# A two-layer attention kernel: the second layer's first key block in two stages, and two key maxima of each first-layer block moved to another PSUM bank

## What is computed

```python
# cross-attention of the first layer; the second has no mask
q = split_heads(query @ Wq.T + bq)
k = split_heads(context @ Wk.T + bk)
v = split_heads(context @ Wv.T + bv)
scores = einsum('bhqd,bhkd->bhqk', q / 4, k) + (1.0 - mask) * -10000.0
out = einsum('bhqk,bhkd->bhqd', softmax(scores), v)
```

## Time and profile before

| | |
|---|---|
| median of 3 runs | 1073.76 us (1072.72 to 1075.67) |
| the profiled execution's own time | 1068.03 us |
| its span | 1066.3 us |
| first layer's blocks 0 to 12 | 38.0 to 478.45 us |
| second layer's pairs of maxima | 556.69 to 573.85 us |
| second layer's blocks 14 to 27 | 575.90 to about 1013 us |

### The profile page before, as it was taken

One profiled execution on the slowest core, in us unless ns is written; L12 is line 12 of the kernel. 1 busy time (PEld: TensorE's weight loads), 2 busy tenths in 40 slices (PEclk: granted clock), 3 DMA queues, 4 the chain that ended last, 5 costly groups with the idle time before them and its releaser, 6 DMA issues. The chain is left out here.

```text
span 1066.3 us, 30777 instructions
## 1 busy us (share of the span) xinstructions
PE 1017.6 (95%) x12921; PEld 687.8 (65%) x12921; DVE 743.1 (70%) x1715; ACT 679.0 (64%) x953; POOL 420.8 (39%) x374
## 2 busy tenths in 40 slices
PE   8899999999999999998878899999999999999876
PEld 5466666676666666665544566667676666666665
DVE  4888888888888888876357666556665565566465
ACT  3677777777778777876542555566556666555722
POOL 4368888888888988881000000101100101000000
PEclk9999999999999999999998999999999999999999
DMA  8420122201221112112031010111100111000000
GB/s 313 140 71 20 54 70 71 67 23 53 71 72 34 45 65 70 53 66 93 10 120 68 2 36 2 37 36 37 36 8 30 37 37 36 2 2 2 2 1 5
DMA packets 14682, 53.31 MB, mean 50 GB/s; under 512 B 3025, under 2 KB 4817, under 8 KB 13649
## 3 DMA queue, kind: packets, MB, share of 16 engines
q1 hardware_dynamic: 14544, 51.35, 14.0%
HBM read 51.21 MB, written 0.13 MB: 48 GB/s over the span
## 5 line engine op out<-in xcount | busy, mean ns | idle before, releaser
L756 DVE TENSOR_REDUCE tile_max<-ps_max 128x1 f32<-128x448 f32 x339 | 200.7, 620 | 150.7 <-PE ps_max L1081 146.5
L753 DVE CUSTOM_DVE_ANT_0 unread<-ps_max,masks 128x448 bf16<-128x448 f32 x396 | 231.4, 621 | 67.4 <-PE ps_max L1081 66.2
L426 POOL TENSOR_TENSOR probs<-probs,masks 128x512 f32<-128x512 f32 x182 | 228.1, 1275 | 72.0 <-ACT probs L539 70.5
L551 ACT ACTIVATE probs<-ps_scores 128x1024 f32<-128x1024 f32 x193 | 187.2, 1021 | 86.2 <-PE ps_scores L1122 86.1
L546 ACT ACTIVATE probs<-probs 128x1024 f32<-128x1024 f32 x196 | 207.4, 1058 | 54.5 <-DVE probs L811 45.7
L1122 PE MATMUL ps_scores<-q_pad,k_full 32*128 32x256 f32 x3088 | 230.6, 377 | 0.0
L1139 PE MATMUL ps_out<-probs,values 128*32 128x128 f32 x6272 | 214.5, 277 | 0.7 <-ACT probs L551 0.4
L1139 PEld LDWEIGHTS ps_out<-probs,values 128*32 128x32 f32 x6272 | 159.4, 110 | 51.7 <-issue 48.0
L1122 PEld LDWEIGHTS ps_scores<-q_pad,k_full 32*128 32x128 f32 x3088 | 191.4, 186 | 0.7
L1081 PE MATMUL ps_max<-k_high,q_high 32*128 32x448 bf16 x735 | 180.1, 358 | 7.9 <-DVE tile_max L756 5.3
L1064 PE MATMUL ps_proj<-ctx_t,wk 128*128 128x448 f32 x384 | 168.8, 562 | 0.0
(11 more groups left out here) (258 smaller groups left out, 914.4 us busy)
## 6 DMA issues: line engine op xcount, KB each, us to landing
ctx_t<-in_ctx_t SPq DMA_DIRECT2D x28, 896.0 KB, 5.3
masks<-in_mask_n SPq DMA_DIRECT2D x14, 448.0 KB, 3.4
masks<-in_mask_t SPq DMA_DIRECT2D x14, 448.0 KB, 3.5
room_w<-in_L_attn_f_w SPq DMA_DIRECT2D x2, 1024.0 KB, 7.5
room_w<-in_L_ffn_w SPq DMA_DIRECT2D x2, 1024.0 KB, 8.8
room_w<-in_L_ffn_w_gate SPq DMA_DIRECT2D x1, 1024.0 KB, 10.6
room_w<-in_L_ffn_w_up SPq DMA_DIRECT2D x1, 1024.0 KB, 13.1
room_w<-in_L_ffn_w_down SPq DMA_DIRECT2D x1, 1024.0 KB, 15.0
```

The costliest lines, as they stand in the source:

```text
L426: nc.gpsimd.tensor_tensor(p, p, three(mask_t[m % 2], TILES)[:, t, :].unsqueeze(1).to_broadcast([P, 4, P]), ALU.add).then_inc(sig("bias_add ...
L551: nc.scalar.activation(prob(T, half), scores_half(T, half), ACT.Exp).then_inc(sig(f"exp_done{half}"), 1)
L753: ins = v.tensor_tensor_reduce(unread[:, j % 2, :], max_bank(m, j)[:, 0:HALF], mask_n[m % 2][:, HALF * half:HALF * (half + 1)], 1.0, -3e38 ...
L756: ins = v.tensor_reduce(tile_max[:, h, half:half + 1], max_bank(m, j)[:, 0:HALF], AX_X, ALU.max)
```

## The change

1. **Two stages in block 14.** `SPLIT` = 3: tiles 0 to 2 (384 keys) are a stage of their own, tiles 3 to 6 the next. The order of block 14's maxima is changed so that all heads' products with the first half of the keys (448 keys, which hold the first three tiles) come first. Only these, eight pairs, run before the first scores; a pair is now two heads with the same half. The other sixteen follow one by one in tiles 0 and 1 (3, 3, 2 a tile), then a second `chain` (end of tile 1) and `turn_max`/`rows_out` (tile 2), before tile 3's scores. The stage's sums go through `sums_out`, `turn_sums` and `add_sums` in tiles 3 and 4. Block 15's maxima are made in tiles 2 to 5 (9, 9, 8, 6), and block 16's as before. Where three maxima lie behind the scores, the first uses `ps_proj`. The counts of stages (`stage`, `tiles_to`, `STAGES_OF`) take the place of the counts of blocks in the waits. The idle matmuls among the pairs are left out.
2. **First layer.** One maximum behind the weighing is taken out of tile 0 and out of tile 2, and one is put behind the scores of tile 5 and of tile 6, in `ps_proj`. DVE reads these two after it has added the mask (`late_bank`, `before_mask`). In block 12, which makes no maxima in tile 6, and in block 0, whose tiles 0 to 5 have counts of their own, only a part of this applies.

```diff
+SPLIT = 3
...
+        def stage(m, t=0):
+            return m + int(m > NB or m == NB and t >= SPLIT)
+
+        def in_stage(m, t):
+            return t - SPLIT if m == NB and t >= SPLIT else t
+
+        def tiles_to(s):
+            return TILES * (s + 1) if s < NB else TILES * NB + SPLIT if s == NB else TILES * s
...
+        STAGES_OF = ((0, NB), (NB, BLOCKS + 1))
...
+        def chained(m, t):
+            return NB + 1 if m == NB and t == SPLIT - 2 else stage(m + 1) if t == CHAIN_AT and m % NB + 1 < NB else None
+
+        def rowed(m, t):
+            return NB + 1 if m == NB and t == SPLIT - 1 else stage(m + 1) if t == ROWS_AT and m % NB + 1 < NB else None
...
-            return c, half, zz, g
+            return (half, c, zz, g) if m == NB else (c, half, zz, g)
...
-        SCORED_AT = ((2, 0, 2, 1, 2, 0, 0), (2, 1, 2, 2, 2, 2, 2))
-        WEIGHED_AT = ((1, 2, 1, 2, 1, 2, 2), (0, 2, 1, 1, 0, 1, 0))
+        SCORED_AT = ((2, 0, 2, 1, 2, 1, 1), (2, 1, 2, 2, 2, 2, 2))
+        WEIGHED_AT = ((0, 2, 0, 2, 1, 2, 2), (0, 2, 1, 1, 0, 1, 0))
+
+        def late_bank(m, t):
+            return m < NB and t >= LAST_AT
+
+        def before_mask(m, t, count):
+            return 0 if late_bank(m, t) else count if m == 0 or m >= NB else min(count, 1)
...
+            if m == NB:
+                own = (3, 3, 2) if t < SPLIT - 1 else own
+                now = ((0, 0, 0), (0, 0, 0), (3, 3, 3), (3, 3, 3), (2, 3, 3), (3, 3, 0), (0, 0, 0))[t]
...
-                            if m > 0 and k == 0 and len(here) == 2 and i == 0 and (t != SUMS_AT or m == NB):
+                            if i == 0 and (two or k == 0 and (late_bank(m, t) or m == NB and t == TILES - 1) or len(here) == 3):
                                 MAX_BANK[to, j] = 2
...
-                    for i in range(H):
+                    for i in range(H // 2):
                         pair_maximum(NB, i)
                         if i in BESIDE_AT:
                             beside_in(BESIDE_AT.index(i))
-                        elif i > 5:
-                            idle_products(1, ps_out)
```

More of the change, by code:

```diff
@@ L187, in count_at @@
             l, n = divmod(m, NB)
-            now, ahead = (0, 0, 0), (0, 0, 0)
+            own, now, ahead = (0, 0, 0), (0, 0, 0), (0, 0, 0)
             first, middle = SCORED_AT[l][t], WEIGHED_AT[l][t]
[L190 to L194, removed]
+            if m == NB:
+                own = (3, 3, 2) if t < SPLIT - 1 else own
+                now = ((0, 0, 0), (0, 0, 0), (3, 3, 3), (3, 3, 3), (2, 3, 3), (3, 3, 0), (0, 0, 0))[t]
+            elif n == 0:
+                now = (2, 2, 2) if t < LAST_AT else (0, 2, 0) if t == LAST_AT else now
+            elif n + 1 < NB and t <= LAST_AT:
+                now = (first, middle, 2 if t < LAST_AT else 0)
             if n + 2 < NB:
                 ahead = (0, 0, 2) if t == LAST_AT else (first, middle, 2) if t > LAST_AT else ahead
-            return now, ahead
+            return own, now, ahead
         MAXIMA, MAX_BANK, MAX_AFTER = {}, {}, {}
         for l in range(2):
-            done, read = {NB * l: 2 * H}, {bank: 2 * H * (NB * l + 1) for bank in range(2)}
+            done = {NB * l: (2 * H, H)[l]}
+            read = {bank: 2 * H * NB * l + (2 * H, H)[l] for bank in range(2)}
             turn_of = 0
@@ L869, in _ @@
                             bias_first(m, t)
-                        for k, j in behind_scores[len(early):]:
+                        for k, j in behind_scores[early:]:
                             maximum(k, j)
-                        if t == SUMS_AT and n > 0:
-                            add_sums(m - 1)
+                        if in_stage(m, t) == SUMS_AT and stage(m, t) > STAGES_OF[l][0]:
+                            add_sums(stage(m, t) - 1)
                         if m == BLOCKS - 1 and t == SUMS_AT:
@@ L1080, in maximum, with pair_maximum @@
                     pe.wait_ge(sig("max_free"), MAX_AFTER[m, j])
[L1081 to L1088, removed]
+                product(m, j, max_bank(m, j))
+            def pair_maximum(m, i):
+                if i == 0:
+                    pe.wait_ge(sig("k_high"), 2 * m + 2)
+                if i == 2:
                     pe.wait_ge(sig("q_copied"), 4)
[L1090 to L1093, removed]
+                need("max_free", 2 * H * m + 2 * (i - 2))
+                for k in range(2):
+                    product(m, 2 * i + k, pair_bank(i)[:, k, :])
             def scores(m, t):
                 T = TILES * m + t
+                if in_stage(m, t) == 0:
+                    pe.wait_ge(sig("max_copied"), stage(m, t) + 1)
                 if t == 0:
-                    pe.wait_ge(sig("max_copied"), m + 1)
                     pe.wait_ge(sig("k_copied"), 4 * m + 4)
@@ L1117, in scores @@
                     rows = slice(32 * g, 32 * (g + 1))
-                    mm(banks[g], minus16[rows, :], max_rows[m % 2][rows, :], start=True, stop=True)
+                    mm(banks[g], minus16[rows, :], max_rows[stage(m, t) % 2][rows, :], start=True, stop=True)
                 for c in range(DC):
```

103 lines of the change are left out of this document (58 added, 45 removed).

## The result

The changed kernel takes 1061.85 us in the median of six runs (1060.48 to 1066.93) against 1073.24 us (six runs) before. The comparison gives a ratio of 0.9909 (not the quotient of the two medians, which is 0.9894), with a 95% interval of 0.9884 to 0.9935. That is faster, as forecast, but by about three times the forecast amount: 1070.0 us was expected, and the range ended at 1063.5. The profiled execution took 1060.48 us, with a span of 1058.7 us.

A forecast was written before the change was run, and what follows sets the result against it. PE was taken to bound the first layer's tiles, DVE those of the second layer's first block. Minus 5.6 plus 1.9 gave minus 3.7 us against the 1073.76 us median: 1070.0 us, range 1063.5 to 1078.0.

The forecast's parts named there:

- The second part: Second layer's first block: shorter head minus 8.6, longer tiles plus 4.5, falls of the clock plus 6.0, sum plus 1.9 us.
- First layer, minus 5.6 us.: Blocks 0 to 12: tiles 0 and 2 save 0.38 us each, tile 6 pays 0.29; minus 5.6 us in all.
- Rivals 3 and 4: First layer: 3, late ACT exponential cancels gain, 1079.2 us, chance 0.09; 4, half the tiles' gain, 1074.6 us, chance 0.18.
- The head, minus 8.6.: Before block 14's first scores: eight of sixteen paired maxima leave, saving 8.6 us.
- Tiles with eight take 5.1 us and with nine 5.7: Block 14's tiles, bound by DVE: times by number of maxima at full clock, block 36.4 us, plus 4.5.
- I take two falls, 6.0 us: Block 14: the clock falls twice to its lower level, 10 us and 3.0 us of cost each, plus 6.0 us.
- Rival 1: Block 14: no fall of the clock, second part minus 4.1 us, whole kernel 1064.1 us; chance 0.20.
- Rival 2: Block 14: lower clock holds through tiles 1 to 6, costing 13.8 us, whole kernel 1077.9 us; chance 0.08.

The follow-up runs named there:

- two_banks: Changed kernel, but block 14's groups of three maxima behind the weighing and ahead of the next tile use two banks, not three: 1063.45 us, one run.
- filled: Changed kernel plus idle PE products before the maxima are turned and behind five later maxima of block 14's tile 0: 1060.92 us, ratio 0.9895.
- threes_0_4: Changed kernel, first layer: tile 4's maximum behind the weighing goes behind its scores, tile 6's behind tile 0's scores: 1065.49 us, ratio 0.9940.
- stages_only: Changed kernel with the first layer's tables of before, so only block 14's two stages: 1067.74 us, ratio 0.9948.

## Why the prediction was wrong

The direction was right, but only the first layer carried it for the reason given. The second part was forecast to cost 1.9 us and gains 3 to 4 us at the same clock.

**First layer, minus 5.6 us.** Right. Blocks 1 to 11 are 0.44 us shorter (forecast 0.47), block 12 0.78 (0.76), block 0 0.33 longer (0.29, in the executions without a fall there): minus 5.3 us. Alone it measures minus 6.3 us with an interval that holds this. The sizes were off against each other. Tiles 0 and 2 gave 0.48 and 0.41 us instead of 0.38 each: besides the product's own 0.29 us, the scores no longer lose time behind the two products ahead of them, as shown above. Tile 6 paid 0.34 (0.29). Tile 1 grew by 0.12: ACT's exponential of tile 0 did fit, but its copy of the keys did not. PE turns the old sums into the bank that this copy empties (249.12 + 0.64 = 249.76), and waited for it:

```profile
249.12 0.64 ACT L543 ACTIVATE k_full<-ps_proj,bk 128x448 f32<-128x448 f32 x1
```

```profile
249.82 0.42 PEld L1195 LDWEIGHTS ps_proj<-ident,out_t 128*128 128x128 f32 x4 [0.36 <-ACT k_full L543]
```

Rivals 3 and 4 fall.

**The head, minus 8.6.** It is minus 9.4 us. Left out: a pair is now two heads, whose products lie in different rows of the array. The first four start together, DVE's first read follows them after 0.53 us instead of 0.69, and it starts its third read without the 0.43 us it idled before:

```profile
554.26 0.37 PE L1112 MATMUL ps_scores<-k_high,q_high 32*128 32x448 bf16 x4 [0.69 <-ACT q_high L618]
```

Before, four took 0.93 us:

```profile
556.00 0.93 PE L1092 MATMUL ps_scores<-k_high,q_high 32*128 32x448 bf16 x4 [0.69 <-ACT q_high L581]
```

Another 0.17 us lies between the chain and the first scores. No run separates the new pairing from the left-out idle matmuls; this account is read from the two timelines.

**"Tiles with eight take 5.1 us and with nine 5.7".** This step failed, in two ways. I read the condition on three products as holding behind the scores only, while it gives every group of three, in all three places, a third bank; tile 3 then has no idle time of DVE at all, nine reads in 5.03 us. And I took 0.59 us for a read, 2.96 us divided by five, though one gap lies within those five. Back to back, reads are 0.54 us apart in the kernel before too: (2.23 minus 0.62) / 3 from the last DVE row. With 0.54 the same working gives 5.0 for eight, which is what was measured, and 5.55 for nine; `two_banks` gave 5.48 and the third bank takes it to 5.03. At full clock block 14 is about 34.5 us (4.98, 4.91, 5.00, 5.03, 5.62, 5.04, 3.85) instead of 36.4: 1.9 us of the error. Two of these tiles never ran at full clock in a profile of the changed kernel itself: tile 1 is from `filled`, tile 6 from `threes_0_4`, which make block 14's maxima in the same order.

**"I take two falls, 6.0 us".** This step failed too, and is a little the larger. In the sum it counted 2.3 us, since the 31.89 us set against it held 3.7 us of low clock of the kernel before. Two falls were right for the first profile, but they cost 2.1 us there and in stages_only, and 5.4 in the second. The step was wrong in kind as well. I charged the changed kernel with falls and compared with an execution of before that had been lucky with its own: its head and its block 0 kept the full clock, though in another execution they lost 4.5 and 2.8 us. The 5.7 us between that profile and the median go with such falls, and I carried them over as a constant. Between kernels with the same mean clock the fair sum has no term for it.

**The sum by what was measured**: at full clock before's block 14 is 28.1 us (its tiles of 3.96, five of about 4.1 or less, and 3.84; its tile 1 was never free of a fall and is taken to be like its neighbours). Minus 5.3, minus 9.4, plus 34.5 minus 28.1 = plus 6.4, minus 0.3 in block 15: minus 8.6 us. Both comparisons of the changed kernel hold this: minus 9.8 us (minus 12.5 to minus 7.0) and minus 11.3 us (minus 15.0 to minus 7.4). My own sum made so would have been minus 5.6, minus 8.6, plus 8.3 = minus 5.9 us. At the same mean clock the estimate is minus 10.0 us; what lies between it and minus 8.6 stays open.

Rival 1 names a time, 1064.1 us, nearer to the measured one than the forecast, but by luck: its condition, no fall, was not met in any profile, and its 36.4 us for the block were too many by 1.9. Rival 2 did not decide, since the clock came back in every profile and the mean was the same in both kernels (0.988). What the Trainium skill says of a clock that goes back and forth (TensorE: Matmul & The Clock Gate, section "A second HAM failure mode: psum-queue depth-cycling") agrees with this trace: in block 14 of the changed kernel's first profile it fell and returned twice.

## What to carry to other kernels

Before costing a stretch that two engines hand back and forth, list the bank of every product from the plan itself, not from the condition's first reading: one more bank in the rotation, or one read put behind a long operation, changed tiles by 0.3 to 1.5 us here. When a row gives one time for several instructions, look for a gap inside it before dividing. Where the granted clock falls at different places from run to run, compare stretches at full clock, and take the low clock's share from the runs' mean clocks, not from one profile. A median that lies above its profile is no constant to add.

## What the runs showed of the hardware

- The granted clock of a program that does not change falls at different places in different executions, 25 us of low clock a run on average. In the kernel before this moved block 0 between 35.6 and 38.4 us and the stretch before block 14 between 78.2 and 82.7 us. A fall at block 14's tile 1 came in all twelve profiles without added matmuls, and in neither of the two with them.
- Products of 32 rows that start together in different rows of the array cost PE little more than one (four in 0.37 us). Four that lie in the same rows took 0.93 us. One alone, between work on all rows, costs 0.29 us.
- DVE's reads of 448 columns from PSUM follow each other after 0.54 us, on two banks as on three. A third bank saved 0.45 us at most in a tile of nine by letting DVE read while PE makes scores.
- A high busy time of PE by the records does not mean the full clock: PE was busy 9.11 of 10 us in a stretch at the lower level.
